# A fused layer on eight cores: zero-tile matmuls at the start, constants on another queue, weights in quarters, softmax in slot 0

## The reference

```python
xn = (x - mean) / sqrt(var + 1e-5)                    # LayerNorm, no gain
q, k = phi(xn @ W_Q.T), phi(xn @ W_K.T)               # phi = elu + 1, 8 heads of 64
v = xn @ W_V.T
S = g*S + k_t v_t^T ; z = g*z + k_t                   # per step, g = sigmoid(decay)
y = (S q / (z.q + 1e-6)) * sigmoid(xn @ W_g.T + b)    # linear attention, gated
out = x + y @ W_O.T                                   # W_O: 1024 x 512
scores = softmax(xn @ gate_w.T)                       # router over 8 experts, top 2
out += xn @ W_lin.T + b_lin + sum_top2 score*(xn @ left[e]) @ right[e]   # rank 4
```

## Time and profile before

| what | value |
|---|---|
| median of 3 runs | 261.59 us (261.10 to 263.84) |
| the profiled execution's own time | 263.04 us |
| span of its slowest core (core 5) | 262.0 us |
| TensorE busy | 238.8 us, 91% |
| VectorE busy | 162.4 us, 62% |
| ScalarE busy | 76.0 us, 29% |
| GpSimd busy | 61.7 us, 24% |
| read from memory, written to it | 32.00 MB, 8.39 MB |

### The profile page before, as it was taken

The page is one execution under the profiler, slowest core; times in us unless marked ns, Lnnn a source line. Parts: engine busy times, 40 slices in busy tenths (PEclk is TensorE's granted clock), DMA queues, the critical chain, the costliest instruction groups (busy, mean ns, idle before and its releaser), DMA issues.

```text
span 262.0 us, 5276 instructions; the slowest of 8 cores (258.1 to 262.0 us)
## 1 busy us (share of the span) xinstructions
PE 238.8 (91%) x1688; PEld 117.4 (45%) x1688; DVE 162.4 (62%) x425; ACT 76.0 (29%) x128; POOL 61.7 (24%) x99
## 2 busy tenths in 40 slices
PE   0348999999897999999999999999999999999995
PEld 0223454454453555444454555444545454445442
DVE  5365457658857657666566657557566776687522
ACT  2563765576163323312322021111111201000000
POOL 2761100011134230505050402112214030333000
PEclk9999999999999999999999999999999999999999
DMA  6999999999986226352327232233222224343423
GB/s 174 207 175 255 251 169 206 233 181 180 245 219 102 83 60 184 101 155 67 118 78 129 83 101 83 88 94 103 81 100 83 101 83 124 136 140 108 159 104 136
DMA packets 20366, 35.86 MB, mean 137 GB/s; under 512 B 12210, under 2 KB 12530, under 8 KB 20084
## 3 DMA queue, kind: packets, MB, share of 16 engines
q1 hardware_dynamic: 17444, 24.89, 32.9%
q0 software_dynamic: 2896, 10.64, 21.5%
HBM read 32.00 MB, written 8.39 MB: 154 GB/s over the span
## 4 chain that ended last, share of the span: by engine, by line
PE 84%; DVE 6%; DMA 4%; issue 3%; ACT 1%; SPq 0%; DVEq 0%; ACTq 0%
PE PJ L365 26%; PE L L387 17%; PE L L431 9%; PE PJ L358 7%; PE PJ L387 4%; PE L L365 4%; DMA x_sb<-x 4%; PE PJ L431 2%; PE L L358 2%; PE T L336 2%; PE SY L379 2%; PE SY L403 2%; PE T L344 1%; PE T L417 1%; PE SY L407 1%
## 5 line engine op out<-in xcount | busy, mean ns | idle before, releaser
L387 PE MATMUL L<-wlin_sb,xnfm 128*128 128x512 bf16 x208 | 49.2, 379 | 0.0
L323 POOL TENSOR_SCALAR S_blk<-S_sb,small_s 128x260 bf16<-128x260 f32 x30 | 28.6, 969 | 82.7 <-DVE S_sb L814 82.5
L387 PEld LDWEIGHTS L<-wlin_sb,xnfm 128*128 128x128 bf16 x208 | 20.0, 98 | 24.1 <-issue 0.8
L885 ACT ACTIVATE e_sb<-PJ 128x512 bf16<-128x512 f32 x28 | 16.5, 594 | 41.2 <-PE PJ L365 39.7
L643 DVE TENSOR_SCALAR e_sb<-e_sb 128x512 bf16<-128x512 bf16 x32 | 9.7, 303 | 30.0 <-ACT e_sb L885 30.0
L861 ACT ACTIVATE xn_tm<-x_sb,nmr,rstd 128x1024 bf16<-128x1024 f32 x16 | 19.9, 1245 | 25.4 <-POOL nmr L279 23.8
L431 PE MATMUL L<-wo_sb,ygfm 128*128 128x512 bf16 x104 | 26.7, 379 | 0.0
L365 PE MATMUL PJ<-xnfm,wq_sb 128*128 128x512 bf16 x112 | 26.6, 380 | 0.0
L365 PE MATMUL PJ<-xnfm,wg_sb 128*128 128x512 bf16 x112 | 26.6, 379 | 0.0
L365 PE MATMUL PJ<-xnfm,wk_sb 128*128 128x512 bf16 x112 | 26.6, 380 | 0.0
L358 PE MATMUL PJ<-wv_sb,xnfm 128*128 128x512 bf16 x96 | 24.6, 400 | 0.0
(11 more groups left out here) (116 smaller groups left out, 339.0 us busy)
## 6 DMA issues: line engine op xcount, KB each, us to landing
ro_sb<-x SPq DMA_DIRECT2D x16, 512.0 KB, 4.0
out<-ro_sb SPq DMA_DIRECT2D x15, 512.0 KB, 2.7
x_sb<-x SPq DMA_DIRECT2D x10, 512.0 KB, 9.1
x_sb<-x POOLq DMA_DIRECT2D x6, 512.0 KB, 20.5
wlin_sb<-wlin POOLq DMA_DIRECT2D x1, 2048.0 KB, 38.0
wv_sb<-wv POOLq DMA_DIRECT2D x4, 256.0 KB, 11.8
wq_sb<-wq POOLq DMA_DIRECT2D x2, 512.0 KB, 17.6
wk_sb<-wk POOLq DMA_DIRECT2D x2, 512.0 KB, 24.4
```

The costliest lines, as they stand in the source:

```text
L323: GP.tensor_scalar(S_blk[:, :].rearrange("p (q w) -> p q w", q=4)[:, :, 65 * e : 65 * e + 65], S_sb[:, :].rearrange("p (q w) -> p q w", q= ...
L387: TE.matmul(lb(c, n)[:, :], xnk(k, c), wlin_sb[:, D * k + 512 * n : D * k + 512 * n + 512], start=False, stop=False)
L885: SE.activation(e_sb[:, 512 * (n % 2) : 512 * (n % 2) + 512], bank[:, :], AF.Exp).then_inc(ac_e, 1)
```

## The change

Constants: `ident`, `small` and `cmat` become one array `cst` (128 x 467 float32), loaded by one DMA on ScalarE's queue, followed there by chunk 2 of x. VectorE copies `ident` and `small` out of it, ahead of `stats(1)`.

TensorE: `warm(n)` issues n 128x512 matmuls on `S_blk`, which VectorE now clears before all else. There are 22 before the first transposition, 6 after it, 3 and 4 between pieces of the V projection.

Scalars of chunks 1 and 3 come from GpSimd's `rs`. GpSimd issues the weights after VectorE's clearings, no longer after chunk 0 of x. All four projection weights go by quarters, over six banks. TensorE's opening order is rewritten.

`top2b(0)` and `stats(9)` move behind masks and state of slot 0; `xn(9)` and `rs(9)` follow.

```diff
-        SY.dma_start(ident[:, :], ident_d[:, :]).then_inc(d_id, 16)
-        load_x(2)
         load_x(3)
-        SY.dma_start(small[:, :], small_d[:, :]).then_inc(d_sm, 16)
-        SY.dma_start(cmat, cmat_d[:, :]).then_inc(d_cm, 16)
...
-        SY.wait_ge(d_wg[1], 16)
+        SY.wait_ge(d_wg[3], 16)
         load_x(10)
...
+    def wload_q(dst, srcd, i, s):
+        o = 2 * FH * i
+        GP.dma_start(dst[:, o : o + 2 * FH], srcd[:, o : o + 2 * FH]).then_inc(s[i], 16)
...
     def pool_program():
         GP.memset(mhalf[:, :], -0.5).then_inc(po_ini, 1)
-        GP.wait_ge(d_x[0], 16)
+        GP.wait_ge(po_ini, 1)
+        GP.wait_ge(dv_ini, 3)
         for i in range(4):
+            wload_q(wv_sb, wv_d, i, d_wv)
+        rs(1)
+        wload_q(wq_sb, wq_d, 0, d_wq)
+        wload_q(wq_sb, wq_d, 1, d_wq)
         xload(4)
+        rs(3)
+        wload_q(wq_sb, wq_d, 2, d_wq)
...
         rs(8)
-        rs(9)
         for c in range(NCH):
-            if c + 10 < NCH:
+            if c + 10 < NCH and c >= LAG:
                 rs(c + 10)
...
+            if c == 0:
+                rs(9)
+            if c < LAG:
+                rs(c + 10)
...
+    ring6 = [PJ[0], PJ[1], L[0], L[1], SYb[0], SYb[1]]
+    vb = [ring6[i] for i in (0, 1, 2, 3, 2, 0, 5, 2)]
+    qb = [ring6[i] for i in (4, 5, 0, 1)]
+    kb = [ring6[i] for i in (3, 4, 5, 2)]
+    gb = [ring6[i] for i in (3, 4, 0, 1)]
...
+    def warm(n):
+        for _ in range(n):
+            TE.matmul(SYb[1][:, :], S_blk[:, 0:128], S_blk[:, 0:512], start=True, stop=True)
...
     def pe_program():
+        TE.wait_ge(dv_z, 1)
+        warm(22)
+        TE.wait_ge(dv_id, 1)
         xtr(0)
+        warm(6)
         xtr(1)
         TE.wait_ge(dv_xev, 1)
+        TE.wait_ge(d_wv[0], 16)
+        vproj(0, vb[0], 0, 2)
+        warm(3)
+        TE.wait_ge(d_wv[1], 16)
+        vproj(0, vb[0], 2, 4)
+        warm(4)
+        TE.wait_ge(dv_xev, 2)
+        vproj(1, vb[1], 0, 4)
         xtr(2)
+        TE.wait_ge(d_wv[2], 16)
+        for c in range(2):
+            vproj(c, vb[c], 4, 6)
         TE.wait_ge(dv_xev, 3)
+        vproj(2, vb[2], 0, 6)
+        xtr(3)
+        TE.wait_ge(d_wv[3], 16)
+        for c in range(3):
+            vproj(c, vb[c], 6, 8)
         TE.wait_ge(dv_xev, 4)
+        vproj(3, vb[3])
+        for i in range(4):
+            TE.wait_ge(d_wq[i], 16)
+            if i == 3:
+                xtr(4)
+            for m in range(4):
+                if i == 0 and m >= 2:
+                    TE.wait_ge(ac_v, m - 1)
+                fproj(wq_sb, 0, m, qb[m], pe_q, 2 * i, 2 * i + 2)
+        TE.wait_ge(dv_xev, 5)
+        TE.wait_ge(ac_v, 3)
+        vproj(4, vb[4])
...
     def dve_program():
+        VE.memset(S_blk[:, :], 0.0).then_inc(dv_z, 1)
...
         stats(0)
+        VE.wait_ge(d_cm, 16)
+        VE.tensor_copy(ident[:, :], cst[:, 403:467].bitcast(BF16)).then_inc(dv_id, 1)
+        VE.tensor_copy(small[:, :], cst[:, 384:403]).then_inc(dv_sm, 1)
         stats(1)
...
         stats(8)
         top2a(0)
-        stats(9)
...
-        top2b(0)
         VE.wait_ge(po_dk, 1)
         for c in range(NCH):
...
+            if c == 0:
+                top2b(0)
             if more:
                 phi(8 + 2 * c, PJ[0], fm(qfm, b + 1)[:, 512 * s : 512 * s + 512], dv_q)
...
+            if c == 0:
+                stats(9)
             if c + 10 < NCH and lo < 0:
                 stats(c + 10)
...
     def act_program():
         SE.wait_ge(dv_one, 1)
         SE.activation(dum[:, :], one_c[:, :], AF.Exp)
+        SE.dma_start(cst, cst_d[:, :]).then_inc(d_cm, 16)
+        SE.dma_start(xc(2), x_d[256:384, :]).then_inc(d_x[2], 16)
```

More of the change, by code:

```diff
@@ L46, in build_core @@
     blin_d = din("blin", [1, D])
[L47 to L49 removed]
+    cst_d = din("cst", [128, 467])
     out_d = nc.dram_tensor("out", [T, D], F32, kind="ExternalOutput").ap()
@@ L508, in pe_program @@
[L508 to L512, removed]
-            fproj(wk_sb, 0, m, ring4[(m + 2) % 4], pe_k, 0, 4)
-        TE.wait_ge(d_wk[1], 16)
-        for m in range(4):
-            fproj(wk_sb, 0, m, ring4[(m + 2) % 4], pe_k, 4, 8)
-        xtr(6)
-        TE.wait_ge(dv_xev, 6)
-        xtr(7)
-        TE.wait_ge(d_wg[0], 16)
-        for m in range(4):
-            TE.wait_ge(dv_k, m + 1)
-            fproj(wg_sb, 0, m, ring4[(m + 2) % 4], pe_g, 0, 4)
@@ new lines, in pe_program @@
+        TE.wait_ge(ac_v, 3)
+        vproj(4, vb[4])
+        for i in range(4):
+            TE.wait_ge(d_wk[i], 16)
+            if i == 3:
+                xtr(5)
+            for m in range(4):
+                if i == 0 and m == 0:
+                    TE.wait_ge(ac_v, 4)
+                elif i == 0 and m < 3:
+                    TE.wait_ge(dv_q, m)
+                elif i == 0:
+                    TE.wait_ge(ac_v, 5)
+                fproj(wk_sb, 0, m, kb[m], pe_k, 2 * i, 2 * i + 2)
+        TE.wait_ge(dv_xev, 6)
@@ new lines, in pe_program @@
+        TE.wait_ge(dv_q, 3)
+        vproj(5, vb[5])
+        for i in range(4):
+            TE.wait_ge(d_wg[i], 16)
+            if i == 3:
+                TE.wait_ge(dv_xev, 7)
+                TE.wait_ge(dv_k, 3)
+                vproj(6, vb[6])
+                xtr(7)
+            for m in range(4):
+                if i == 0 and m < 2:
+                    TE.wait_ge(dv_k, m + 1)
+                elif i == 0 and m == 2:
+                    TE.wait_ge(ac_v, 6)
+                elif i == 0:
+                    TE.wait_ge(dv_q, 4)
+                fproj(wg_sb, 0, m, gb[m], pe_g, 2 * i, 2 * i + 2)
+            if i == 1:
+                xtr(6)
@@ L528, in pe_program @@
         TE.wait_ge(d_lg, 16)
         tgp(0)
-        for c in (6, 7):
-            TE.wait_ge(dv_xev, c + 1)
-            TE.wait_ge(ac_g, c - 5)
-            vproj(c, L[c - 6])
+        TE.wait_ge(dv_xev, 8)
+        TE.wait_ge(dv_k, 4)
+        vproj(7, vb[7])
         for c in range(NCH):
@@ L546, in pe_program @@
                 TE.wait_ge(dv_norm, c)
+            else:
+                TE.wait_ge(ac_g, 2)
+                TE.wait_ge(ac_v, 7)
             scores(c)
@@ L630, in stats @@
         VE.wait_ge(dv_st, c + 1)
-        if c < 8:
+        if c < 8 and c not in (1, 3):
             VE.tensor_scalar(nm[:, c : c + 1], mv[:, 2 * c : 2 * c + 1], -1.0, None,
@@ L740, in dve_program @@
         stats(4)
-        stats(5)
         xev_v(4)
-        for m in range(2):
-            phi(m, ring4[m], fm(qfm, 0)[:, 512 * m : 512 * m + 512], dv_q)
+        for m in range(4):
+            if m == 2:
+                stats(5)
+            phi(m, qb[m], fm(qfm, 0)[:, 512 * m : 512 * m + 512], dv_q)
+        stats(6)
         xev_v(5)
-        for m in range(2, 4):
-            phi(m, ring4[m], fm(qfm, 0)[:, 512 * m : 512 * m + 512], dv_q)
-        stats(6)
+        for m in range(4):
+            phi(4 + m, kb[m], fm(kfm, 0)[:, 512 * m : 512 * m + 512], dv_k)
         stats(7)
-        VE.wait_ge(ac_mk, 1)
+        xev_v(6)
+        VE.wait_ge(ac_dec, 3)
         qt(0)
-        for m in range(4):
-            phi(4 + m, ring4[(m + 2) % 4], fm(kfm, 0)[:, 512 * m : 512 * m + 512], dv_k)
-        xev_v(6)
         xev_v(7)
@@ L841, in xn @@
     def xn(c):
-        if c < 8:
+        if c < 8 and c not in (1, 3):
+            j = {0: 0, 2: 1}.get(c, c - 2)
             SE.wait_ge(dv_st, c + 1)
```

125 lines of the change are left out of this document (47 added, 78 removed).

## The result

| kernel | median us | profiled execution | its span | ratio to before, 95% interval |
|---|---|---|---|---|
| before | 261.35 | 263.04 | 262.0 (core 5) | |
| changed | 266.72 (266.21 to 268.50, 4 runs) | 268.50 | 267.3 (core 4) | 1.0192 [1.0158, 1.0227] |

The forecast was 258.0 us, faster; the change makes the kernel 1.9% slower, outside the range of 255.3 to 261.5 us. In one execution each of b1, d2 and d3 the cores of one die ran at a granted clock of 0.81 to 0.89 and took 282.8 to 302.6 us; times and ratios here leave such executions out (with it, b1's median is the 260.34 us that an expectation names).

The account below looks back on a forecast made before the run. TensorE ends last, so it bounds the kernel. Slot 1's start moves from 71.83 to 67.2 us; with the remaining 190.2 the span is 257.4, profiled time 258.4, expected median 258.0 us, range 255.3 to 261.5.

Parts of the forecast that it names:

- rival C: Front: zeros don't lift the clock, or (second form) gaps lose it again; slot 1 at 73.1, time 264.3 us; chance 0.14.
- Constants and x2 on ScalarE's queue: Opening loads: table usable at 8 us (7 to 11), chunk 1 transposable at 12.6 instead of 11.3 us.
- Zero-tile matmuls: Before and within the V stage: they hold the clock up, so slow matmuls go at half price, 3.4 us less on core 5.
- V weights earlier: V stage: weights issued 1.6 us earlier, last quarter landing at 18.7 instead of 20.2 us; stage ends at 23.5, not 29.62.
- Weights in quarters over six banks: Q, K, G stage: keeps its 30.9 us, slot 0 starts at 54.4 us, 3.9 us of cover for the weights.
- Router softmax and statistics into slot 0: Slot 0: VectorE's chain grows to 12.8 us from 11.3, so slot 1 starts at 67.2 us.
- What is late next: Slot 0: chunk 10's load lands at 62.9 us, VectorE asks at 63.7, 0.8 us of cover (bounds -1.5 to +2).
- rival B: Slot 0's end: chunk 10's load decides, slot 1 starts 3.1 us behind it; span 257.8 to 258.8, time 259.3 us; chance 0.22.

Follow-up runs that it names:

- b1: The kernel before with zero-tile matmuls alone (22, 8 and 14 around the first two transpositions); 260.20 us, ratio 0.9929.
- d2: The changed kernel with softmax, chunk 9 and chunk 2's queue as before, and V(6) behind the router's matmuls; 263.31 us, ratio 1.0040.
- d3: The kernel before with 27, 8, 8 zeros, bias and chunk 9's statistics ahead of the router's copy, chunks 10 and 11's behind the gate; 259.29 us.
- a2: The changed kernel with chunk 2 of x issued on SP's queue between chunks 1 and 3, as before; 264.16 us, ratio 1.0079.
- c4: The changed kernel with GpSimd's weights again waiting for chunk 0 of x; 264.89 us, ratio 1.0116.
- a1: The changed kernel with router softmax and chunk 9's statistics, scalars and normalisation back ahead of slot 0; 265.75 us, ratio 1.0138.
- b2: The kernel before with router softmax and everything of chunk 9 moved into slot 0, alone; 265.17 us, ratio 1.0117.
- c2: b1 with the bias remainder and the statistics of chunk 9 ahead of the router's copy; 259.77 us, ratio 0.9928.
- d1: The changed kernel with softmax, chunk 9, chunk 2's queue as before, transpositions 6 and 7 earlier, chunk 9's statistics and bias before router's copy; 262.23 us.

## Why the prediction was wrong

Two things failed in the front of the kernel: the constants and chunk 2 came later than I had worked out, and the gaps lost the clock again, rival C's mechanism in its second form. Core 6 kept its clock, so it shows my steps without that, and core 4 shows the whole.

| step | forecast | core 6 | core 4 |
|---|---|---|---|
| V starts | 14.5 | 15.60 | 19.13 |
| V stage ends | 23.5 | 25.37 | 31.83 |
| Q, K, G stage | 30.9 | 30.80 | 30.59 |
| slot 0 | 12.8 | 13.29 | 13.29 |
| slot 1 | 11.3, in the 190.2 | 12.21 | 12.87 |
| from slot 2 | 178.9, in the 190.2 | 178.7 | 178.7 |
| span | 257.4 | 260.4 | 267.3 |

(V's forecast start is chunk 2's statistics, 13.8 us, and the copy of chunk 0.) Of core 4's 9.9 us over the forecast, 8.3 stand in the V stage: 4.6 us of late start, and 3.7 us of length, 2.9 of which core 6 does not have. So the late loads weigh more than the clock.

*Constants and x2 on ScalarE's queue: the failed step.* I took 8 us for the table, with bounds of 7 to 11; it landed at 8.4 to 10.6 us though issued 1.4 us earlier than I assumed, inside the bounds, but the sum went on with 8 alone, an estimate that no row of ScalarE's queue stood behind: chunk 1's statistics began at 10.87 and not 8.3 us on core 4. Worse, I left the statistics of chunk 2 at their times of before, ending at 13.8 us, while moving its load behind 233.5 KB and behind chunk 3: it came at 12.7 to 16.3 us instead of 9.7 to 12.2, and on core 4 its statistics ended at 17.97 us. That is the wait of 2.97 us ahead of the first V matmul. The trace has the table 8.7 us on the way on core 4, and the first loads of all profiles landed in order of issue, whatever their queue. What the late place of chunk 2 costs is a2's 2.6 us.

*Zero-tile matmuls.* That zeros lift the clock was right (b1). That the first 22 leave the first transposition at 9 us was an estimate: in the changed kernel they took 6.5 to 7.8 us and were done by 9.7 us, and the transposition stood at 9.3 to 11.1 us, on seven of eight cores after a wait for the copy of `ident` or for chunk 0's normalisation. That they hold it was wrong: the numbers 22, 6, 3 and 4 fill none of the holes of 2.5 and 3.0 us. The prediction's own times left one: from the first transposition, due at 9 us, to chunk 1's at 12.6 us, a transposition and six zeros fill 1.7 of 3.6 us. I overlooked it. Seven of eight cores lost the clock for a part of the V stage, and the zeros placed there then cost 0.43 us each, on the path. I had also measured the gain at the slowest core: V ended at 29.62 us on core 5, but at 26.6 in the median and 24.7 at best, so there were 3 us less to win on half the cores than the 6.1 that I subtracted.

*V weights earlier.* I had the last V quarter land 1.5 us sooner, at 18.7 us; it landed at 19.3 us (20.4 before, medians), but V did not wait for it, and c4 shows a loss of 1.8 us (266.72 to 264.89; the intervals just part at 1.0158 and 1.0152).

*Weights in quarters over six banks.* The stage's length held (30.8 us), and no weight was late. What I costed at nothing was V(6) moved ahead of the router's matmuls, 1.7 us less cover for VectorE. The softmax's own move hid this in the changed kernel; it showed when a1 put the softmax back.

*Router softmax and statistics into slot 0.* Forecast 12.8 us, measured 13.29 (b2: 13.0): right. Missing were two followers in slot 1: transposition 9 waits 0.76 us for ScalarE's copy `thr`, which now stands behind `xn(9)` and `xn(10)`, and after TensorE's idle time of 0.46, 1.03 and 2.13 us in slot 0 the clock was lost on five of eight cores (0.7 us more in slot 1). b2 alone costs 1.2% where this step as I had it costs 1.5 us, 0.6%.

*What is late next.* Chunk 10 did not decide, since slot 0 came late; on five cores of b1, three of c2 and five of d1 it did, with the 3.1 us from landing to slot 1 of rival B (the rows that the prediction names for them, 68.87 to 71.83, give 2.96).

## What to carry to other kernels

Before a load is moved to another queue, look at what stands behind its first reader in that engine's list: here one late chunk held the copy of an earlier one. Look also at when each load is issued, since here the first loads landed in that order across queues. Count warm-up matmuls against the holes as they are after the change: here they paid where they filled them (b1, 0.7%), and where holes of 2.1 to 3.0 us stayed (the changed kernel), zeros behind them cost 0.43 and not 0.216 us each on seven of eight cores. When the order of one engine changes, ask which other engine's work the old order had covered: here V(6) covered a part of VectorE's 6.4 us. And a gain is sized on every core, not on the slowest alone.
